# Cross attention in rounded passes: queries and head products, sums over partitions on GpSimd, head outputs accumulated in PSUM

## The reference, cut to what matters

```
x = x + cross(layernorm(x), ctx)      # 16 heads of 128
x = x + quantised_attention(...)      # the five other layers follow

def cross(inputs_q, inputs_kv):
    q = (inputs_q @ Wq).reshape(b, 256, 16, 128) * (1 / sqrt(128))
    k = (inputs_kv @ Wk).reshape(b, 4096, 16, 128)
    v = (inputs_kv @ Wv).reshape(b, 4096, 16, 128)
    attn = softmax(einsum('bqhd,bkhd->bhqk', q, k))
    return einsum('bhqk,bkhd->bqhd', attn, v).reshape(b, 256, 2048) @ Wo
```

## Time and profile before

| | before |
|---|---|
| median of 3 runs | 1637.32 us (1635.33 to 1638.84) |
| the profiled execution | 1636.64 us, span 1634.4 us |
| TensorE busy | 1607.9 us, 98% |
| VectorE busy | 1093.6 us, 67% |
| ScalarE busy | 703.9 us, 43% |
| GpSimd busy | 167.9 us, 10% |
| mean granted TensorE clock | 0.998 |

### The profile page before, as it was taken

One profiled execution on the slowest core, in us unless ns is written; L12 is line 12 of the kernel. 1 busy time (PEld: TensorE's weight loads), 2 busy tenths in 40 slices (PEclk: granted clock), 3 DMA queues, 4 the chain that ended last, 5 costly groups with the idle time before them and its releaser, 6 DMA issues.

```text
span 1634.4 us, 22632 instructions
## 1 busy us (share of the span) xinstructions
PE 1607.9 (98%) x8766; PEld 1258.1 (77%) x8766; DVE 1093.6 (67%) x1742; ACT 703.9 (43%) x941; POOL 167.9 (10%) x233
## 2 busy tenths in 40 slices
PE   9999999999999999999999999999999999999998
PEld 8887888888888888888888888887857757544544
DVE  4445787777778778777777779999583762633333
ACT  4334454454445454444444445655341361322221
POOL 0001000000100000010000001111100072011110
PEclk9999999999999999999999999999999999999999
DMA  7876655554565555465454454334320517489994
GB/s 238 228 228 188 161 134 158 151 145 122 172 163 142 149 142 154 118 185 142 113 139 126 133 136 123 93 102 135 137 92 39 206 52 304 183 255 418 421 425 174
DMA packets 125513, 282.93 MB, mean 173 GB/s; under 512 B 7712, under 2 KB 83680, under 8 KB 119264
## 3 DMA queue, kind: packets, MB, share of 16 engines
q1 hardware_dynamic: 103104, 200.75, 38.7%
q0 software_dynamic: 22304, 80.75, 16.4%
HBM read 206.99 MB, written 74.48 MB: 172 GB/s over the span
## 4 chain that ended last, share of the span: by engine, by line
PE 83%; DVE 8%; DMA 3%; issue 3%; ACT 2%; POOL 0%; SPq 0%; DVEq 0%; ACTq 0%; POOLq 0%
PE bank L478 19%; PE bank L41 19%; PE bank L448 17%; PE bank L500 6%; PE bank L2172 5%; PE bank L499 3%; PE bank L2211 2%; PE bank L1738 2%; PE bank L2197 2%; PE bank L1752 1%; PE bank L526 1%; DVE S L830 1%; PE bank L2201 1%; DVE e_parts L851 1%; PE bank L2157 1%
## 5 line engine op out<-in xcount | busy, mean ns | idle before, releaser
L478 PE MATMUL bank<-wv_parts,cT_hi 128*128 128x512 f32 x1024 | 333.7, 389 | 1.5 <-DMA wv_parts<-wv_dram 1.4
L478 PEld LDWEIGHTS bank<-wv_parts,cT_hi 128*128 128x128 f32 x1024 | 192.2, 188 | 41.8 <-DMA wv_parts<-wv_dram 1.8
L851 DVE TENSOR_TENSOR e_parts<-S,e_parts 128x1024 fp32r<-128x1024 f32 (+1 forms) x129 | 156.8, 1215 | 84.7 <-ACT e_parts L656 82.6
L448 PE MATMUL bank<-cT_hi,wk_hi 128*128 128x512 f32 x512 | 204.6, 400 | 0.0
L647 ACT ACTIVATE S<-S 128x1024 f32<-128x1024 f32 (+1 forms) x129 | 135.9, 1053 | 152.7 <-DVE S L830 152.2
L448 PE MATMUL bank<-cT_lo,wk_hi 128*128 128x512 f32 x512 | 199.8, 390 | 0.0
L448 PE MATMUL bank<-cT_hi,wk_lo 128*128 128x512 f32 x512 | 199.7, 390 | 0.0
L478 PE MATMUL bank<-wv_parts,cT_lo 128*128 128x512 f32 x512 | 199.3, 389 | 0.0
L656 ACT CAST e_parts<-S 128x1024 fp32r<-128x1024 f32 (+1 forms) x129 | 134.8, 1045 | 135.1 <-PE bank L500 128.9
L843 DVE TENSOR_TENSOR esum<-esum,S 128x512 f32<-128x512 f32 x210 | 145.0, 691 | 71.7 <-ACT S L647 68.1
L803 DVE TENSOR_TENSOR mx<-mx,S 128x512 f32<-128x512 f32 x222 | 152.9, 689 | 12.8 <-ACT S L641 9.0
(11 more groups left out here) (300 smaller groups left out, 2661.9 us busy)
## 6 DMA issues: line engine op xcount, KB each, us to landing
w<-in_w_moe SPq DMA_DIRECT2D x32, 2304.0 KB, 14.0
v_dram<-v_out SPq DMA_DIRECT2D x112, 512.0 KB, 4.9
v_back<-v_dram POOLq DMA_DIRECT2D x110, 512.0 KB
ctx_nat<-in_ctx SPq DMA_DIRECT2D x8, 1024.0 KB, 5.1
ctx_raw<-in_ctxT SPq DMA_DIRECT2D x7, 1024.0 KB, 8.5
v_dram<-v_back SPq DMA_DIRECT2D x14, 512.0 KB, 4.8
v_late<-v_dram POOLq DMA_DIRECT2D x14, 512.0 KB
wv_parts<-wv_dram POOLq DMA_DIRECT2D x6, 1024.0 KB, 8.3
```

The costliest lines, as they stand in the source:

```text
L448: t = e.matmul(banks[b][:], l, r, start=(c == 0 and m == 0), stop=(c == DT - 1 and m == 2))
L478: t = e.matmul(banks[b][:], l, r, start=(c == 0 and m == 0), stop=(c == DT - 1 and m == 2))
L851: e.tensor_tensor(lo, S[:, of_chunk(j, m), :], hi.bitcast(F32), ALU.subtract).then_inc(e_split, 1)
```

## The change

It does these things, all in the cross attention:

- The queries of all heads and the output products of heads 0 to 11 are made in three rounded passes. ScalarE rounds and VectorE splits the weights (`round_qo`, `split_qo`), the normalised x once (`round_x`, `split_x`), and the head's output (`round_o`, `split_o`). The products of heads 12 to 15 with Wo stay plain.
- The row sums of heads 0 to 13 go to GpSimd (`add_sums`, a sum over partitions like the one for the maximum). VectorE inverts the 128x256 result and scales `oT` with it (`scale_o`, chunk 2).
- With the scaling done ahead of the product, heads 0 to 13 accumulate in the two y banks, and x gets them by two additions in head 14 (`add_heads`). Heads 14 and 15 are added as before.
- `xT_lo` lies where x lies and `xT_hi` where xT lies; x is loaded from DRAM again in head 14.
- The running maximum and the running sum are 128x256 tiles in heads 0 to 11 (the maximum of head 12 too), updated by four dependent operations a chunk in place of two of 128x512, and GpSimd reads them without a fold. The maximum of heads 13 to 15 is a 128x1024 tile, one operation a chunk, folded by one reduction.
- Places: `finish_head(h-1)` moves to the end of chunk 4, `project_q(h+2)` to the end of chunk 7. The query product uses the banks of the value tiles. The splits of Wo and `oT` are in chunk 3, that of Wq in chunk 6. In the late heads `split_k` of chunks 2 and 7 stands ahead of `keep_max`.

The core of the diff:

```diff
         def tensor_cross(e):
             def project_q(h):
-                e.wait_ge(wqo_in, qo_value["wq", h])
...
+                e.wait_ge(qo_split, TT + parts_value["wq", h])
...
-                matmuls(e, banks[Q_BANK][:, 0:T], [(wq_raw[:, c, :], xT[:, c, :]) for c in range(DT)]).then_inc(q_projected, 1)
+                if h >= 2:
+                    e.wait_ge(v_split, units(h - 2, NCH - 1)[0] if h < LATE + 2 else QUADS * KVT)
+                matmuls(e, q_bank(h)[:, 0:T], three_pass([((wq_hi[:, c, :], wq_lo[:, c, :]), (xT_hi[:, c, :], xT_lo[:, c, :]))
+                                                          for c in range(DT)])).then_inc(q_projected, 1)
...
             def finish_head(h):
                 e.wait_ge(o_moved, h + 1)
-                if h < XH - 1:
+                if h == SUMMED:
                     columns_of_sums(h, slice(0, P))
...
                 for i in range(TT):
-                    t = e.matmul(banks[Y_BANKS[i]][:], oT[:, i * P:(i + 1) * P], wqo_raw[:], start=True, stop=True)
+                    tokens = slice(i * P, (i + 1) * P)
+                    if h < LATE:
+                        terms = three_pass([((oT_hi[:, tokens], oT_lo[:, tokens]), (wqo_hi[:], wqo_lo[:]))])
+                    else:
+                        terms = [(oT[:, tokens], wqo_raw[:])]
+                    for n, (l, r) in enumerate(terms):
+                        t = e.matmul(banks[Y_BANKS[i]][:], l, r, start=(n == 0 and (h == 0 or h >= SUMMED)), stop=(h >= SUMMED - 1))
...
-                    if j == 0 and h and starts_quad(h):
-                        finish_head(h - 1)
                     for u in units(h, j):
                         project_v(u)
                     scores(h + 1, j)
-                    if j == 0 and h and not starts_quad(h):
+                    if j == NCH // 2 and h:
                         finish_head(h - 1)
-                    if j == NCH // 2:
+                    if j == NCH - 1:
                         project_q(h + 2)
...
+            def scale_o(h):
+                e.wait_ge(sum_ready, h + 1)
+                own.done(e.reciprocal(esum_t[:], esum_t[:]))
+                own.wait(e)
+                e.wait_ge(o_moved, h + 1)
+                e.tensor_tensor(oT[:], oT[:], esum_t[:], ALU.mult).then_inc(scaled, 1)
...
+                    if j == 2 and h:
+                        scale_o(h - 1)
+                    if j == 3 and h:
+                        split_qo("wo", h - 1)
+                        split_o(h - 1)
+                    if j == NCH - 2:
+                        split_qo("wq", h + 2)
...
+            def add_sums(h):
+                if h < LATE:
+                    e.wait_ge(e_summed, summed(h, NCH - 1))
+                else:
+                    e.wait_ge(sum_folded, folded(h))
+                if h:
+                    e.wait_ge(scaled, h)
+                e.partition_all_reduce(esum_t[:], esum[:] if h < LATE else mx[:], P, bass.bass_isa.ReduceOp.add).then_inc(sum_ready, 1)
...
+                    if j == NCH - 1 and h < LATE:
+                        add_sums(h)
+                    if j == 0 and LATE < h < XH - 1:
+                        add_sums(h - 1)
```

285 lines of the change are left out of this document (193 added, 92 removed).

## The result

The changed kernel takes 1687.29 us (median of 5 runs, 1685.62 to 1688.51), the kernel before in the same series 1637.49: a ratio of 1.0304, 95% interval 1.0293 to 1.0315. That is 50 us more, where 33 were forecast. The profiled execution's span is 1685.1 us, 50.7 over before's 1634.4, at the same clock.

What follows compares the result with a forecast made beforehand. TensorE was taken to bound the plain heads, VectorE nearly binding the late ones. Stops of 49.4 us less 15.1 of relief gave +34, so 1670 us; forecast 1658 to 1680 (chance 0.62), range 1640 to 1688.

Steps and rivals of the forecast that it cites:

- TensorE's relief: Rounded query products (1.43) and head products (1.37) and dropped column sums save TensorE 15.1 us if nothing waits.
- The price of a stop: Scores that had to wait take 1.69 instead of 1.43, so a stop costs 0.26 on top of the wait.
- The reciprocal and the stops of chunks 3 and 4: Reciprocal (1.755) and product make VectorE late: TensorE stops 1.5 in chunk 3 and, with the wo and oT splits, 0.7 in chunk 4.
- VectorE's idle time lies inside its own chain: VectorE waits 1.13 before each esum for an exponential its own subtraction releases; work elsewhere cannot use that time.
- The turn: Between plain heads, the lost cover of the head's products and three narrow sums stop TensorE 1.0 before weighing 0.
- The foldings: Four dependent 256-column operations replace two of 512: +0.35 twice a chunk, costing nothing in steady chunks.
- grows by the two foldings to 1.8: Heads 4 and 8, chunk 1: the chain from v_out to k_lo stops TensorE 1.1 now, 1.8 after.
- Rival C: GpSimd's sum stops VectorE in chunk 7: some 1.2 in twelve heads, +14, 1684 us; chance 0.14 together with another rival.
- the split of wq in chunk 6 leaves it 0.4 late, just within what is in hand: Plain heads, chunk 6: VectorE ends 0.4 late after this split, with no stop of TensorE counted.
- The late heads: Heads 12 to 14: stops of 0.5 at scores 0, 1.4 at weighing 0, 1.4 at scores 4; 7.5 us in all.
- at the start: Start of the kernel: xT and wq are split while VectorE waits for wv to land, +0.3 us.

Runs made afterwards that it cites:

- Run 1: Changed kernel without the reciprocal of the 14 first heads, the output multiplied by the sum itself: 1664.15 us.
- Run 3: Changed kernel, heads 1 to 11: reciprocal, product and output splits moved into VectorE's gaps before sums of exponentials, wq split behind wk's in chunk 7: 1662.75 us.
- Runs 4: Changed kernel with the split of the exponentials ahead of their sum in chunk 0 of heads 1 to 10: 1692.67 us.
- run 7: Kernel before the change with only the narrow foldings of maximum and sum added: 1646.49 us.
- run 9: Changed kernel without the reciprocal, GpSimd's sum a write of ones, the splits of wq (from the third head), wo and oT cut to 2 columns: 1642.63 us.
- 5: Changed kernel with the added work in VectorE's gaps and also chunk 0's split of the exponentials ahead of their sum: 1668.59 us.
- run 2: Changed kernel with GpSimd's sum over the partitions replaced by a write of ones, same waits and signal: 1676.10 us.
- run 11: Kernel of Run 3 with the head's end one chunk later and GpSimd's sum behind the next head's maximum: 1762.23 us.
- runs 6: Kernel of Run 3 with the split of the output's weights back at the end of chunk 3: 1663.87 us.
- 12: Kernel of Run 3 with the head's end one chunk later and the wq load issued ahead of chunk 6's spill: 1663.83 us.

## Why the prediction was right in its direction and short in its size

The measured 1687.29 lies 0.7 under the upper end of the range, 1688, and outside the 1658 to 1680 that had the chance of 0.62. The mechanism, VectorE's lateness at `k_lo` and at the turn, was the right one; the size was short by 17 us, and that the range still holds it is in part luck.

**TensorE's relief** was right: the blocks of query products last 1.41 to 1.42 (1.43 forecast), the heads' products 1.38 to 1.39 (1.37). PE's busy time on the page fell by only 0.7 all the same. In the plain head from 510.38 it is 70.33 for 70.39, though the relief is 1.1: a stop is 0.16 longer from block to block than in the brackets, which is time shown as busy, and the scores behind a stop take 0.1 more. Four stops and three such blocks make about 0.95.

**The price of a stop** was misread: "a stop costs 0.26 on top of the wait". The 1.69 of the earlier trace rows at 442.80 runs to the end of the last product, the 1.43 beside it to the start of the next block. From start to start these twelve products take 1.53, as they do in the changed kernel.

**The reciprocal and the stops of chunks 3 and 4**, the largest term: forecast 1.5 and 0.7 (+0.37 with a half of wv), measured 1.33 and 0.65 (+0.32), each with 0.1 in the scores behind it. The reciprocal takes 1743 ns in the mean, by the row 1755. Run 1 took it out and both stops went but for 0.28 in chunk 4. My reason, that VectorE's idle time lies inside its own chain where other work can't use it, needs a limit: it is so for the order as written. Run 3 puts the same work there and gets 24.5 us back.

**The turn** was right: 1.0 forecast, 0.95 measured. Runs 4, 7 and 9 show that it takes what the forecast named, the lost cover and the longer sum, both. Runs 4 and 5 show that it can't be bought off by an exchange.

**The foldings** were right for plain heads (nothing, run 7). For the quads' first heads the step "grows by the two foldings to 1.8" is too small where nothing else stops, 2.7 by blocks in run 7; in the changed kernel, where the scores of chunk 0 have already waited 1.56, it is 1.3. Such a head was to get 4.4 longer net (5.5 of stops less 1.1 of relief) and got 6.0 longer (78.1 for 72.1); 1.0 of the difference is the stop in chunk 7.

**Rival C was half true**, and this is the step that failed: "the split of wq in chunk 6 leaves it 0.4 late, just within what is in hand". That sum had no place for GpSimd, whose addition takes 1.74 where the forecast read the maximum's 1.06. With the clash the split takes 1.23 to 1.79, and TensorE stops 0.67 in chunk 7, 0.93 with a half of wv. With the slower scores this is 10.1 us in 12 heads. The first 12 heads lasted 38.8 us longer (139.7 to 1027.6 against 139.3 to 988.4), the forecast's terms give 29.3 there; the difference of 9.5 is about this stop. Taking the sum away gave 11 (run 2, the late heads' clash among them). I had treated the clash as a case of its own (14 us more, or nothing) and had the split apart from it; in fact the two stand one behind the other. The Trainium skill, "SBUF — State Buffer", section "Who interferes with whom", names this lock between a VectorE operation with two SBUF inputs and a GpSimd operation that reads SBUF. The traces agree in the kind: `wqo_lo`, `e_parts` and the subtraction, all with two SBUF inputs, grow by 0.5 to 1.1, 0.5 to 0.9 and 0.9 beside a sum of 1.74 to 1.85, return to 0.68 and 1.22 without it, and `k_lo` with its PSUM input stays at 0.69 beside it (run 11). They differ in the length: the same page of the Trainium skill, in "SBUF: two separate sides", has whichever of the two starts first hold the pair for its whole instruction, and here the sum keeps its 1.74 and the VectorE operation ends as if freed 0.9 to 1.0 us into it, also where it had begun 0.2 us first.

**The late heads** were under-sized, 7.5 of stops forecast. Two late heads lasted 7.7 us longer already, net, where the terms give 3.2. Two sizes were off: the maximum's fold reads 1024 strided elements and takes 2.01, where I took the 1.22 of an operation that reads PSUM; and the first subtraction takes 2.12 for 1.22 beside GpSimd's sum. The stop before the first scores of head 14 is 1.9 (0.5 forecast), and one of 0.72 ahead of the queries, where wk and wq are split in that order, was not in it at all. Weighing 0 and chunk 4 were right, 1.5 and 1.37 for 1.4 each.

**The last turn** is a step that I left out. TensorE waits for the folded sum of head 14, which stands behind the maximum's folds on VectorE, in before and after:

```profile
1132.63 0.58 PE L514 MATMUL bank<-ones_col,esum_t 128*128 128x1 f32 x4 [1.97 <-DVE esum_t L870]
```

```profile
1182.00 0.99 PE L540 MATMUL bank<-ones_col,esum_t 128*128 128x1 f32 x4 [3.85 <-DVE esum_t L973]
```

The fold of 1024 elements ahead of it takes 1.94 for the 0.71 of before, and behind the longer wait the column sums and the head's products take 4.40 for 2.79 at a granted clock of 0.50 for 0.80. The span from head 15's first scores to the end, which holds the third late head too, is 3.8 us longer. So 38.8 + 7.7 + 3.8 and 0.4 at the start make 50.7. The forecast's terms, less the relief of each part, are 29.3, 3.2, 2.1 and -0.3: it lacked 9.5 in the first twelve heads, 4.5 in two late heads, 1.7 in the third with the last turn, and 0.7 at the start.

By parts: the reciprocal costs 23 (run 1), GpSimd's sum 11 (run 2), and the rest of 44.7, some 10, are the splits (what run 9 took out less the two; not measured alone). The shares are not independent: run 3 ends the stop of chunk 7 with the sum still there. The narrow foldings cost 9.5 in the kernel before. What remains, some 5 us over before in run 9 with those foldings in it, is the 15 of relief set against the foldings, the turn, the late heads and the last turn.

Run 3's last two late heads took 1.8 us more than those of runs 6 and 12, which have the same code there. That is the clock as well: it is 0.51 from 1057.20 to 1064.20 us in run 3, and weighing 0 and the keys behind it take 2.69 and 3.87; at the same place, behind the same stop of 1.75, it is 1.00 in run 6, and they take 1.46 and 2.73. The 2.4 us of each head are partly paid back, since the stop of 1.4 in chunk 4 is then gone.

```profile
1057.20:1064.20 7.00, 6.05 (x20) 4.92 (x19) 6.30 (x9) 4.07 (x6) 0.55 (x1) 0.51 0.10 28
```

What is still open: why the clock fell there in one run and not in the other; how much of the last turn each of its parts costs, since no run took them apart; and what run 3 would gain with GpSimd's sum where run 11 has it.
